# Two places in place of three for activations, turned rows and product banks, three output-row places in place of four, in an expert stage on one core

## What is computed

```python
router_logits = jnp.einsum('th,eh->te', xf, Wr)
topk_vals, topk_idx = jax.lax.top_k(router_logits, TOP_K)      # TOP_K = 2
routing_weights = jax.nn.softmax(topk_vals, axis=-1)
h = jnp.einsum('th,efh->etf', xf, Wi) + bi[:, None, :]         # 192 -> 768
h = jax.nn.gelu(h, approximate=False)
expert_out = jnp.einsum('etf,ehf->eth', h, Wo) + bo[:, None, :] # 768 -> 192
...
out = jnp.einsum('tk,tkh->th', routing_weights, gathered)
return h + out                                                  # the residual rows
```

## Time and profile before

| what | value |
|---|---|
| timed runs, median of 3 (lowest to highest) | 989.66 us (989.16 to 992.24) |
| span of the profiled execution | 995.9 us |
| time of the profiled execution around its span | not given apart from the span |
| its busy shares: PE, PEld, DVE, ACT, POOL | 87%, 83%, 66%, 54%, 65% |
| the expert stage in it: first and last bias add (L1372) | 515.36 and 979.81 us |
| mean granted TensorE clock | 0.848 of full speed |

### The profile page before, as it was taken

How to read it: one execution, slowest core, us unless ns; L and a number is a source line. 1 busy time by engine, 2 the same in 40 slices (tenths; PEclk the granted TensorE clock), 3 DMA queues, 4 the chain that set the end, 5 groups by cost and what they waited for, 6 DMA issues and landing times.

```text
span 995.9 us, 22850 instructions
## 1 busy us (share of the span) xinstructions
PE 869.3 (87%) x7469; PEld 822.9 (83%) x7469; DVE 656.0 (66%) x2142; ACT 536.0 (54%) x1271; POOL 644.7 (65%) x552
## 2 busy tenths in 40 slices
PE   3959898998898739893889999999999999999993
PEld 2959898998898738892679999999999989898993
DVE  3167857776867565978756776666667656666662
ACT  1222223213312325599667777777777767677761
POOL 6777777777777300100067886777778768788886
PEclk9957556556756669996699999999999999999997
DMA  8437547457465429855946446745744543343454
GB/s 245 131 87 248 179 153 257 136 200 225 157 207 195 126 86 282 225 166 131 245 101 149 61 60 158 191 61 122 199 83 63 130 96 61 59 60 59 61 57 44
DMA packets 99788, 138.31 MB, mean 139 GB/s; under 512 B 13427, under 2 KB 81430, under 8 KB 97654
## 3 DMA queue, kind: packets, MB, share of 16 engines
q0 software_dynamic: 39552, 53.26, 28.1%
q1 hardware_dynamic: 59142, 73.59, 24.3%
q10 hardware_dynamic: 1008, 10.34, 2.8%
HBM read 98.14 MB, written 39.02 MB: 138 GB/s over the span
## 4 chain that ended last, share of the span: by engine, by line
PE 29%; DMA 22%; POOL 22%; issue 12%; DVE 8%; ACT 4%; DVEq 2%; SPq 1%; POOLq 0%; ACTq 0%
DMA out<-Hs,id_s 20%; POOL ev_g L521 13%; POOL emb_g L512 5%; PE bank L799 3%; PE bank L801 3%; PE bank L800 3%; POOL blob L537 3%; PE bank L780 2%; PE bank L781 2%; PE bank L784 2%; PE bank L783 2%; PE bank L782 2%; DVE hstats L1157 2%; ACT adj_s L956 1%; PE bank L763 1%
## 5 line engine op out<-in xcount | busy, mean ns | idle before, releaser
L975 ACT ACTIVATE Hs<-bank,U 128x256 bf16<-128x256 f32 x426 | 214.0, 502 | 126.0 <-PE bank L784 126.0
L551 POOL DMA_INDIRECT out<-Hs,id_s x142 | 233.5, 1645 | 65.6 <-issue 45.6
L537 POOL DMA_INDIRECT blob<-xtab_d,id_g x142 | 151.6, 1068 | 122.7 <-DVEq L1340 79.6
L521 POOL DMA_INDIRECT ev_g<-in_word_emb,ids_i x192 | 189.7, 988 | 58.5 <-issue 57.9
L976 ACT ACTIVATE Hs<-bank,U 128x256 f32<-128x256 f32 x426 | 216.4, 508 | 0.0
L799 PE MATMUL bank<-U,Hs 128*128 128x192 bf16 x852 | 210.0, 246 | 0.3 <-issue 0.3
L801 PE MATMUL bank<-U,Hs 128*128 128x192 bf16 x852 | 208.8, 245 | 0.0
L800 PE MATMUL bank<-U,Hs 128*128 128x192 bf16 x852 | 208.5, 245 | 0.0
L1362 DVE TENSOR_TENSOR Hs<-Hs 128x512 bf16<-128x512 f32 x213 | 146.8, 691 | 92.1 <-ACT Hs L976 92.0
L780 PE MATMUL bank<-wst,U 128*128 128x256 bf16 x426 | 116.6, 274 | 1.3 <-DVE wst L1351 1.3
L781 PE MATMUL bank<-wst,U 128*128 128x256 bf16 x426 | 116.7, 274 | 0.0
(11 more groups left out here) (216 smaller groups left out, 1643.2 us busy)
## 6 DMA issues: line engine op xcount, KB each, us to landing
adj_s<-in_adj SPq DMA_DIRECT2D x48, 256.0 KB, 7.3
ev_g<-kpad_d SPq DMA_DIRECT2D x24, 512.0 KB, 5.8
U<-blob_d SPq DMA_DIRECT2D x14, 771.0 KB, 5.0
wst<-in_wsrc SPq DMA_DIRECT2D x8, 1344.0 KB
blob_d<-blob ACTq DMA_DIRECT2D x7, 1443.0 KB
U<-blob_d SPq DMA_DIRECT2D x14, 672.0 KB, 5.7
xtab_d<-U SPq DMA_DIRECT2D x4, 1552.0 KB, 17.0
out<-Hs SPq DMA_DIRECT2D x4, 1536.0 KB, 12.8
```

The lines of the kernel that those rows point to most:

```text
L521: pool.indirect_dma_start(ev_g[:, p, j, b, :], None, t["word_emb"], bass.IndirectOffsetOnAxis(ap=ids_i[:, 1 + j, i * Q + b:i * Q + b + 1], ...
L537: pool.indirect_dma_start(xg_f[:, q % RX, h, :], None, xtab_d, bass.IndirectOffsetOnAxis(ap=id_g[:, 2 * q + h:2 * q + h + 1], axis=0)).the ...
L551: pool.indirect_dma_start(out, bass.IndirectOffsetOnAxis(ap=id_s[:, 2 * q + h:2 * q + h + 1], axis=0), yo[:, q % RY, h, :], None, compute_ ...
L975: f(hh[w][:, d, :], ps, ACT.Gelu, bias=bi[:, d:d + 1])
```

## The change

W3 becomes 2: `xgT`, `hf`, `hh`, `hl` and the banks of the down product get two places in place of three, and with W3 move the waits that are written with it (for `down` on ACT and DVE, for `biased` on PE). RY becomes 3: `yo` gets three places in place of four. The small routing weights `wk` keep their three places under a name of their own, WK. The parity in the wait of bias_out is left as it is, so the semaphore is still that of q's own parity while the count is now landed_by(q - 3).

```diff
-W3 = 3
+W3 = 2
+WK = 3
...
-RY = 4
+RY = 3
...
-        wk = sb("wk", [128, W3, 2])
+        wk = sb("wk", [128, WK, 2])
...
-                    last = v.tensor_scalar(yo[:, x, h, :], yo[:, x, h, :], wk[:, w, h:h + 1], None, ALU.mult)
+                    last = v.tensor_scalar(yo[:, x, h, :], yo[:, x, h, :], wk[:, q % WK, h:h + 1], None, ALU.mult)
...
-                weights(q, q % W3)
+                weights(q, q % WK)
```

## The result

The changed kernel is slower: 998.14 us (median of 20 runs, 992.86 to 1004.08) against 992.32 us (median of 20, 986.26 to 997.79), ratio 1.0065 with a 95% interval of 1.0046 to 1.0085. By the ratio that is 6.5 us more (4.6 to 8.4), by the two medians 5.8; 8.5 were forecast. More runs moved the median of before from 989.66 to 992.32.

A forecast was written before the change was run, and what follows sets the result against it. POOL, through the four places of yo, was taken to bound the stage. PE's loss of 12.9 us less 4.4 from POOL's shorter tail gave +8.5, on 989.7 us: 998.2 us, range 990 to 1005.

The forecast's parts named there:

- What bounds the stage: Expert stage: POOL holds PE back through the four places of yo; its lag grows in jumps near weight loads.
- Two places cost nothing: hf, hh, hl, xgT and banks: each new wait is covered by one that stays; 0 us, bounds 0 and 7.
- Rival D: Two places do cost, through a misread order: 0.1 us a tile, +15.6 at most; chance 0.12 shared with another rival.
- The odd tiles wait for q-2: bias_out on DVE: the count landed_by(q-3) on the odd semaphore means tile q-2, so odd tiles wait for its scatter.
- Rival E: bias_out: odd tiles wait for q-3, so the cap is 15.2 us; about +2 to +3 us; chance 0.03.
- The cap at 8.6 us: PE stalls for odd tiles once the scatter starts over 8.6 us after its bias add, from tile 17 or so.
- The sum: Whole stage: PE loses 12.9 us, POOL's shorter tail gives 4.4 back; +8.5 us, bounds +2.6 and +10.8; chance 0.62.
- rival B: The lag stays under 8.6 us without the profiler, so odd tiles never hold PE; 0 to +3 us; chance 0.13.
- the one held constant: POOL's pace to tile 63: its scatter still starts at 958.62 us; shift 0, bounds -5.9 (fast) and +2.3 (slow).
- A (POOL runs free): POOL keeps 6.44 us a tile in calm and capped stretches, 9.2 us gained, -0.7 in all; chance 0.10.
- C (more than the tail): PE's stalls hold POOL up again at the weight-load jumps; +14.5 us, 1004 us; chance 0.12 shared with another rival.
- The signs that were named: bias_out's scatter waits grow from 40 to well over 60 us; tile 63's scatter stays within 4 us of 958.6.

The follow-up runs named there:

- the half change: Changed kernel with four yo places and the old wait (RY = 4), two places for the rest; ratio 1.0007 to the kernel before.
- the other half: Changed kernel with W3 = 3: three yo places and the changed wait, three places for the rest; ratio 1.0076 to the kernel before.
- both exchanges of wait and place: Changed kernel with bias_out waiting for exactly q-3: 1.0001; kernel before, all places kept, with only the changed wait: 1.0076; both ratios to the kernel before.
- the pair without reloads: Kernel before and changed kernel, each with reloads of expert weights left out (output not the reference's); ratios 0.9914 and 0.9912 to the kernel before.
- the kernel without waits inside an expert: Kernel before, from tile 13 on the scatter skips waiting for the previous tile's landing where both share an expert; ratio 0.9912 to the kernel before.

## Why the prediction was right

**What bounds the stage.** Right: POOL, through yo. Without most of its waits for the previous tile's landing the stage is 11 us shorter (459.7 for 470.6), as short as without any weight load.

**Two places cost nothing.** Right within the noise, by the half change (1.0007) and by the other half, which has the whole loss. Rival D falls.

**The odd tiles wait for q-2.** Right, shown by both exchanges of wait and place. Rival E falls with them; its own figure, +2 to +3 us for a wait on q-3, can't be told from nothing: 1.0001 was measured, with up to +2.5 us in the interval. Its tail came as worked out, 980.03 - 950.02 = 30.0 us from tile 63's scatter to the last for 27.4 before; in these two profiles POOL's way to tile 63 took it back, 346.3 us for 352.8, the term of the next point but one.

**The cap at 8.6 us.** Right: lags of 7.4 to 8.6 on the held tiles (7.7 forecast) and 8.7 to 9.7 on the even ones, stalls from tile 17 on.

**The sum.** Direction and mechanism right, size somewhat too high: 8.5 against 6.5 (4.6 to 8.4). That the forecast of 998.2 us falls on the measured 998.14 is luck: its base, the median of three runs, was 2.7 us below the later median, and its shift 2.0 to 2.7 us too high. The 6.2 us between span and timed runs, too, were not the profiler's doing, as rival B reads them: the execution was a long one (about 997.7 us, see above).

The term that looks mis-sized is the one held constant, the start of tile 63's scatter. "To 63" is 351.1 us as the mean of the three kernels with the old yo (before twice, two places alone) and 347.2 of the three with the change's wait (after, three yo places, new wait alone): -3.9 us, where 0 was taken and -5.9 was the fast bound. The single values overlap, though (346.9 to 353.5 and 344.9 to 350.2), so this shift is likely and not shown. Against it, tile 63's bias add to tile 70's took 982.78 - 939.87 = 42.91 us and not 41.75, since tile 65 waited again. Together 8.5 - 3.9 + 1.2 = 5.8, and the stage's means, from the same six profiles, are 468.9 and 474.6. In PE's terms it is +9.8 to the last bias add (463.0 to 472.8) and -4.0 for the tail (5.8 to 1.8), where +12.9 and -4.4 were forecast.

Whether and why POOL was quicker isn't settled. In the calm stretch from tile 18 to 24 it was no quicker: 7.04 us a tile in the changed kernel, 6.86, 6.55 and 6.90 in the other three with a wait for q-2, against 6.59. But the third jump is missing: from tile 38 to 42 POOL took 6.79 to 6.86 us a tile in the four kernels with a wait for q-2, and 7.8 to 8.5 in the four that kept the wait for q-4, the reloads and all of POOL's own waits; with the wait for exactly q-3, and so a lag between, it is 7.13. That the lag decides how hard a weight load hits POOL fits this and is not shown.

**Rivals A, B, C.** A (POOL runs free): fell, between the loads it took 6.5 to 7.0 us a tile under the cap. B (the lag is absorbed): falls by the result; that two tiles ahead suffice is true only without the jumps, as the pair without reloads shows. C (more than the tail): not seen.

**The signs that were named.** The odd tiles, tile 17, the lag under 10 and the last scatter 1.8 us after its bias add came as said. PE's waits for row_lo grew by 11.8 us (23.9 for 12.1) where 13 were said, but only 8.7 + 5.6 = 14.3 of them lie between 620 and 820 us. PE never waited for the bias add at the up or down product, and ACT's waits for PE stayed (121.9 us for 119.8 to 960 us). Two signs failed. The waits of bias_out on scatters did not grow: 43.1 us in 26 waits, for 44.0 in 33 before; fewer tiles wait, and in the kernel before many such waits were 1.1 to 1.5 us, of which 0.3 stand before a bias add that waits for nothing and 0.87 are the slack that DVE has the earlier trace rows. And tile 63 lay 947.66 - 512.13 = 435.5 us after the first bias add for 443.3 before, so further off than the 4 us allowed; the profile of two places alone, with the old wait, is nearly as far off (437.5 us), so two single executions can't carry that sign.

## What to carry to other kernels

When a ring of buffers changes from an even to an odd number and its semaphores are split by parity, work out for each parity which event the old expression now names; here one line cost 0.7%, and the buffers themselves nothing that could be measured. A buffer's depth is worth only the lag that builds up behind it, so read the lag tile by tile from the two timelines before cutting one. And ask what makes the lag: here it was a wait on landings that most tiles did not need, and taking it away was worth more (0.9%) than the change had lost (0.7%).

## What was not expected of the hardware

POOL had 0.15 us a tile to spare and hardly used it. Its 6.44 us cycle slides against DVE's 6.59 until one descriptor instruction starts inside a DVE operation that reads two operands from SBUF (row_lo or split_hidden). Then it is stretched in each tile, and the lag is frozen. At 4.7 us without reloads it is the first fetch, which starts with 0.27 us of row_lo left and takes 1.17, tile after tile. At 7.79 from tile 24 to 63 in the kernel without waits inside an expert, it is the scatter of the second half, which starts inside split_hidden and takes 1.71 to 1.76.

The stretch is the time left of the DVE operation less about 0.13 us. In the kernel before, from the first bias add to tile 64's, 35 scatters start inside split_hidden's operation (L1362). With 0.13 us of it left or less they take 1.62 or 1.63, with 0.25 left 1.76, with 0.41 left 1.91, with 0.63 left 2.13. The four that start together with it take only 1.59 to 1.62. And 20 scatters start inside the bias add, which reads one operand from a bank and one from SBUF: with 0.12 to 0.55 us of it left, all take 1.59.

The Trainium skill ("SBUF — State Buffer", § Who interferes with whom) says that a VectorE instruction with two SBUF inputs contends with a GpSimd instruction that reads SBUF. The overlaps agree: operations with two SBUF inputs stretched the issues, the one with a bank input did not. No run took row_lo or split_hidden away, so that the frozen lag comes from it is argued and not shown.
